# Attention on one NeuronCore: the order of turning and weighting on TensorE

## The chip, the cores and the metric

The program runs on one NeuronCore of a Trainium2 chip. The metric is the device time of one execution in microseconds (us). The engines are TensorE (PE: matmuls and transposes; its weight loads are listed apart as PEld), VectorE (DVE), ScalarE (ACT), GpSimd (POOL) and SyncE (SP, which issues most transfers). Each engine runs its own list of instructions in order, and they meet only at semaphores.

## The reference, cut to what matters

Two layers of cross attention and feed-forward on 2 batches of 512 tokens of width 1024, with a context of 1024 positions. The part that the change touches is the first attention, with 32 heads of width 32 in 8 groups of 4:

```python
scores = jnp.einsum('bghnd,bgsd->bghns', query, key) / D_HEAD ** 0.5
scores = jnp.where(mask, scores, jnp.finfo(scores.dtype).min)
attention = jax.nn.softmax(scores, axis=-1)
out = jnp.einsum('bghns,bgsd->bghnd', attention, value)
out = out.transpose(0, 3, 1, 2, 4).reshape(b, n, D_MODEL)
```

Here n is 512 queries, s is 1024 context positions, h the 4 heads of a group, and b and g together make 16 pairs.

## The kernel before

The kernel runs five stages one after the other. Stage B (`stage_b`, from L596) is the attention, in some 545 of the 1222 us. It goes through 256 steps: 16 pairs (`bg`) of 16 steps each, and a step is one tile of 128 queries of one head against all 1024 positions. A body (`body`) has 32 steps, so two pairs; the first and the last body are written out apart, the six between are a loop. A unit is 8 steps.

For step k the engines do this:

- TensorE computes the scores of step k + 2 (`score`, L689): two matmuls of 512 columns into one of two halves of the PSUM tile `psS`. They run two steps ahead. They wait until VectorE has read the scores that this half held (`masked`).
- VectorE (`mask_min`, L809) adds the mask, writes the tile to SBUF and takes the minimum of each row.
- ScalarE (`exponentials`, L763) takes the exponential and the row sum. This gives the probability tile `Pr`.
- TensorE turns the probability tile, 128 queries by 1024 positions, in eight 128x128 transposes (L736) into the PSUM tile `psT`: first the lower four (half 0), then the upper four (half 1).
- ScalarE copies half 0 out of PSUM (`keep` of ScalarE, L771), VectorE half 1 (`keep` of VectorE, L818), both into `PT`. Half f of step k can only be turned when half f of step k - 1 has been copied (`kept[f]`, wait at L734).
- TensorE weights the values (`weigh`, L703) with the turned tiles of the unit before: one eighth of it in each step, as eight matmuls with 32 columns of weights and 256 moving columns, four side by side in the four column strips of the array. Only the first of the eight portions of a unit waits for anything.
- Once for each pair, in its twelfth step, TensorE spreads the reciprocals of the row sums (`spread_rec`, L715, 32 small matmuls) over the PSUM tile of the output. VectorE multiplies by it two steps later (`normalise`, L830).

TensorE's order in a step is: scores of step k + 2 (S), half 0 (T0), the spreading where there is one, weighting (W), half 1 (T1). VectorE's is: `mask_min` of step k + 2, copy of half 1 of step k. ScalarE's is: exponential of step k + 1, copy of half 0 of step k. In the first eight steps there is nothing to weight, and after the last step eight portions of weighting are left over. Scores are written in steps 0 to 253 alone.

Of the kernel before, what the change touches and what calls it, by code (L numbers as in the profile page):

```python
# [595 lines left out]
def stage_b(nc, ident, hand, QHd, QLd, KHd, KLd, Vd, AOd, early, start_early_loads):  # L596
# [4 lines left out]
    with ExitStack() as stack:  # L601
# [8 lines left out]
        UNIT = 2 * HPG  # L610
# [41 lines left out]
        @block.sync  # L652
        def _(sp):
            def store(bg, u):
                sp.wait_ge(AO_ready, bg + 1)
                sp.dma_start(AOd[ds(bg, 1)].rearrange("a p q -> p (a q)"), AOs[:, u, :]).then_inc(stored[u], 16)


            start_early_loads(sp)
            for u in range(2):  # L660
                sp.wait_ge(hand.stored[u], 32 * (KT + B * KVT))
                sp.wait_ge(hand.q2_stored[u], 16 * NK)
            sp.wait_ge(hand.v_stored, 16 * B)
            with sp.Fori(0, BG // 2 - 1) as it:
                for u in range(2):
                    sp.wait_ge(scored, it * BODY + (u + 1) * STEPS)
                    hand.load_scores(sp, QHd, QLd, KHd, KLd, it * 2 + (u + 2), u)
                    sp.wait_ge(weighed, (it * 2 + (u + 1)) * (STEPS // UNIT))
                    hand.load_values(sp, Vd, it * 2 + (u + 2), u)
                    store(it * 2 + u, u)  # L670
            sp.wait_ge(stored[0], 16 * (GROUPS // 2))
            sp.wait_ge(stored[1], 16 * (GROUPS // 2) + 16)
            for t in range(2):
                early.load_attention(sp, AOd, t)
            for u in range(2):
                store(BG - 2 + u, u)
            sp.wait_ge(stored[0], 16 * (BG // 2))
            sp.wait_ge(stored[1], 16 * (BG // 2) + 16)

        @block.tensor  # L680
        def _(pe):
            def score(it, k):

                u, j = divmod(k, STEPS)
                qt, h = divmod(j, HPG)
                if j == 0:
                    pe.wait_ge(qkv_in[u], (it + 1) * (16 * QKV_DMAS))
                for n in range(2):
                    last = pe.matmul(psS[:, k % 2, n * HALF:(n + 1) * HALF], Qs[:, u, h, qt * P:(qt + 1) * P],  # L689
                                     Ks[:, u, n * HALF:(n + 1) * HALF], start=True, stop=True)  # L690
                last.then_inc(scored, 1)

            def weigh(it, k, first=False):

                u, unit, kt = (k // UNIT - 1) // 2 % 2, k // UNIT - 1, k % UNIT
                if kt == 0:
                    pe.wait_ge(kept[0], it * BODY + k)
                    pe.wait_ge(kept[1], it * BODY + k)
                    if unit % 2 == 0 and not first:
                        pe.wait_ge(AO_ready, it * 2 + (u - 1))  # L700
                cols = slice(unit % 2 * UQ, (unit % 2 + 1) * UQ)
                for h in range(HPG):
                    last = pe.matmul(psO[h * DH:(h + 1) * DH, u, cols], Vs[:, u, kt, :], PT[:, unit % 2, kt, h, :],  # L703
                                     start=(kt == 0), stop=(kt == NK - 1))
                if kt == NK - 1:
                    last.then_inc(weighed, 1)

            def spread_rec(bg, u):

                pe.wait_ge(rec_ready, bg + 1)  # L710
                pe.wait_ge(O_kept, bg + 1)
                for qt in range(QT):
                    for h in range(HPG):
                        one = rec[:, u, qt * HPG + h:qt * HPG + h + 1].to_broadcast([P, DH])
                        last = pe.matmul(psO[h * DH:(h + 1) * DH, u, qt * P:(qt + 1) * P], one, ident[:],  # L715
                                         start=True, stop=True)
                last.then_inc(spread, 1)

            def body(it, first=False, last=False):
                for k in range(BODY):  # L720
                    u, j = divmod(k, STEPS)

                    if not (last and k + 2 >= BODY):
                        pe.wait_ge(masked, it * BODY + (k + 1))
                        if k + 2 < BODY:
                            score(it, k + 2)
                        else:
                            score(it + 1, k + 2 - BODY)
                    pe.wait_ge(probs, it * BODY + (k + 1))
                    for f in range(2):  # L730
                        if f == 1 and not (first and k < UNIT):
                            weigh(it, k, first)
                        if not (first and k == 0):
                            pe.wait_ge(kept[f], it * BODY + k)  # L734
                        for kt in range(NK)[PARTS[f]]:
                            last_t = pe.transpose(psT[:, kt, :], Pr[:, k % PR, kt * P:(kt + 1) * P], ident[:])  # L736
                        last_t.then_inc(turned[f], 1)
                        if f == 0 and j == UNIT + 3 and not (first and u == 0):
                            spread_rec(it * 2 + (u - 1), 1 - u)

            score(0, 0)
            score(0, 1)
            body(0, first=True)
            with pe.Fori(1, BG // 2 - 1) as it:
                body(it)
            body(BG // 2 - 1, last=True)
            for k in range(UNIT):
                weigh(BG // 2, k)
            spread_rec(BG - 1, 1)
# [1351 lines left out]
```

## Time and profile before

| what | us |
|---|---|
| median of 3 runs | 1222.91 |
| lowest and highest of them | 1221.82 and 1226.61 |
| the profiled execution, its own time | 1223.41 |
| its span, first to last instruction | 1221.6 |
| PE busy (86%) | 1052.5 |
| DVE busy (74%) | 903.5 |
| ACT busy (54%) | 658.1 |

The page's row of 40 slices shows TensorE at 9 tenths or more from slice 9 to slice 25, which is the attention. A busy time of TensorE counts modelled ends of matmuls that overlap; so what a group of matmuls costs is better read from one start to the next start. A row with "x4" has merged four instructions that followed each other on the engine.

### The profile page before, as it was taken

Reading aid. Unit: us, or ns where it says so; the run is one execution under the profiler, and the core shown is the slowest. Engines: PE = TensorE matmul, PEld = TensorE weight load, DVE = VectorE, ACT = ScalarE, POOL = GpSimd, SP = SyncE. Lnnn points to the kernel's source line nnn. Section 1 sums busy time; section 2 is a strip of 40 time slices with the busy share of each in tenths; the row PEclk is TensorE's granted clock in tenths of the full one; section 3 lists DMA queues with packets and bytes.
Section 4 is the critical chain, followed back from the end, with each engine's and each line's share of the span. In section 5 each row is a group of like instructions: output and inputs, shape, how many; then the busy total and the mean of one; then the engine's idle time right before and its main releaser. Section 6 shows DMA issues by size and latency. Waiting matters only on the chain. (4 is left out here: it accounts for less than half of the span.)

```text
span 1221.6 us, 21150 instructions
## 1 busy us (share of the span) xinstructions
PE 1052.5 (86%) x7371; PEld 744.7 (61%) x7376; DVE 903.5 (74%) x1886; ACT 658.1 (54%) x1127; POOL 126.0 (10%) x99
## 2 busy tenths in 40 slices
PE   6999997999999999999999999799999877522118
PEld 5878876666666666666666666668888633311007
DVE  5854435989898888888989887646533356699997
ACT  4422211888888888888888886412212074534114
POOL 1211103000000000000000000000112055034300
PEclk9999999999999999999999999899999989855559
DMA  8368887412222221122222210834130000000003
GB/s 336 112 223 293 282 226 247 183 41 66 66 61 64 64 64 44 33 55 64 64 64 60 65 49 10 310 101 124 48 122 0 1 0 1 13 0 0 0 0 138
DMA packets 55566, 112.92 MB, mean 92 GB/s; under 512 B 7724, under 2 KB 21164, under 8 KB 55388
## 3 DMA queue, kind: packets, MB, share of 16 engines
q1 hardware_dynamic: 55452, 112.26, 29.7%
q8 instruction: 30, 0.49, 0.2%
q14 instruction: 20, 0.16, 0.0%
q0 software_dynamic: 64, 0.00, 0.0%
HBM read 83.99 MB, written 27.26 MB: 91 GB/s over the span
## 5 line engine op out<-in xcount | busy, mean ns | idle before, releaser
L763 ACT ACTIVATE XS<-XS,b_mins 128x1024 f32<-128x1024 f32 x256 | 294.9, 1152 | 86.8 <-DVE b_mins L809 84.6
L736 PEld LDWEIGHTS b_psT<-ident,XS 128*128 128x128 f32 x2048 | 235.1, 141 | 144.2 <-issue 100.5
L736 PE MATMUL b_psT<-ident,XS 128*128 128x128 f32 x2048 | 322.2, 281 | 0.8 <-ACT b_PT L771 0.2
L809 DVE CUSTOM_DVE_ANT_0 XS<-b_psS,b_mbias 128x1024 f32<-128x1024 f32 x256 | 312.1, 1219 | 1.7 <-PE b_psS L689 0.6
L818 DVE COPY b_PT<-b_psT 128x512 f32<-128x512 f32 x256 | 177.0, 691 | 54.8 <-PE b_psT L736 53.7
L689 PE MATMUL b_psS<-XTh 128*128 128x512 f32 x512 | 186.3, 446 | 6.6 <-PEq L102 5.5
L703 PE MATMUL b_psO<-b_PT,XTh 128*32 128x256 f32 x2048 | 161.8, 390 | 1.2 <-DVE b_PT L818 0.9
L771 ACT COPY b_PT<-b_psT 128x512 f32<-128x512 f32 x256 | 145.3, 567 | 11.8 <-PE b_psT L736 11.8
L689 PEld LDWEIGHTS b_psS<-XTh 128*128 128x128 f32 x512 | 78.3, 193 | 7.9 <-issue 5.9
L703 PEld LDWEIGHTS b_psO<-b_PT,XTh 128*32 128x32 f32 x2048 | 43.0, 108 | 41.7 <-issue 40.8
L1725 PE MATMUL e_psT<-e_XN,e_dg 128*128 x128 | 30.0, 400 | 41.2 <-DVE XR L1980 41.2
L1147 ACT ACTIVATE c_sd<-c_mv,c_eps 128x1 f32<-128x1 f32 x16 | 4.7, 296 | 103.8 <-DVE c_mv L1234 103.8
L1227 DVE TENSOR_TENSOR XR<-XR,c_psM 128x1024 f32<-128x1024 f32 (+1 forms) x16 | 19.5, 1218 | 55.1 <-PE c_psM L1054 55.1
L399 ACT ACTIVATE a_oh<-a_psM 128x512 fp32r<-128x512 f32 x24 | 14.2, 597 | 82.9 <-PE a_psM L322 62.5
L1295 POOL MEMSET c_eps<- 128x1 f32 x1 | 0.1, 100 | 553.0 <-POOLq L601 553.0
L480 DVE SCALAR_TENSOR_TENSOR a_ol<-a_psM,a_oh 128x512 fp32r<-128x512 f32 x24 | 16.5, 690 | 51.7 <-ACT a_oh L399 51.5
L1725 PEld LDWEIGHTS e_psT<-e_XN,e_dg 128*128 128x128 f32 x128 | 25.8, 202 | 45.8 <-issue 41.9
L1709 PE MATMUL e_psP<-ident,e_xp 128*128 128x128 f32 x16 | 5.5, 448 | 52.8 <-POOL e_xp L2014 52.8
L322 PE MATMUL a_psM<-XTh,WTl 128*128 128x512 f32 x128 | 50.8, 397 | 0.0
L322 PE MATMUL a_psM<-XTh,WTh 128*128 128x512 f32 x128 | 50.7, 396 | 0.0
L1054 PE MATMUL c_psM<-WEh,c_Lh 128*128 128x512 f32 x128 | 50.6, 395 | 0.0
L322 PE MATMUL a_psM<-XTl,WTh 128*128 128x512 f32 x128 | 49.9, 390 | 0.0
(224 smaller groups left out, 1732.8 us busy)
## 6 DMA issues: line engine op xcount, KB each, us to landing
XS<-in_ctx SPq DMA_DIRECT2D x16, 512.0 KB, 5.3
XTh<-QHd SPq DMA_DIRECT2D x32, 256.0 KB, 4.7
XTh<-QLd SPq DMA_DIRECT2D x32, 256.0 KB, 5.2
XS<-in_ctx_turned SPq DMA_DIRECT2D x8, 512.0 KB, 12.0
XS<-in_x SPq DMA_DIRECT2D x8, 512.0 KB, 10.4
a_wst<-in_L_xattn_w_q SPq DMA_DIRECT2D x8, 512.0 KB, 5.5
a_xn<-in_ctx_turned SPq DMA_DIRECT2D x8, 512.0 KB, 3.6
QHd<-a_oh SPq DMA_DIRECT2D x16, 256.0 KB, 4.8
```

Of the source, the lines that this page charges most:

```text
L322: last = pe.matmul(psM[:, m % 4, :], a[:, w % 2, k, :], b[:, k, cols], start=(k == 0 and a is WTh and b is mh), stop=(k == KT - 1 and a is ...
L480: dve.scalar_tensor_tensor(out=ol[:, m % 2, :], in0=psM[:, m % 4, :], scalar=inv_root if M_Q <= m < M_V1 else 1.0, in1=oh[:, m % 2, :].bit ...
L689: last = pe.matmul(psS[:, k % 2, n * HALF:(n + 1) * HALF], Qs[:, u, h, qt * P:(qt + 1) * P], Ks[:, u, n * HALF:(n + 1) * HALF], start=True ...
L703: last = pe.matmul(psO[h * DH:(h + 1) * DH, u, cols], Vs[:, u, kt, :], PT[:, unit % 2, kt, h, :], start=(kt == 0), stop=(kt == NK - 1))
L736: last_t = pe.transpose(psT[:, kt, :], Pr[:, k % PR, kt * P:(kt + 1) * P], ident[:])
L763: act.activation(Pr[:, k % PR, :], Sc[:, k % 4, :], ACT.Exp, bias=mins[:, k % 4:k % 4 + 1], scale=-1.0, accum_out=sums[:, u, j:j + 1]).the ...
L771: act.copy(PT[:, (k // UNIT) % 2, PARTS[0], k % HPG, queries(k)], psT[:, PARTS[0], :]).then_inc(kept[0], 1)
L809: dve.tensor_tensor_reduce(out=Sc[:, k % 4, :], in0=psS[:, k % 2, :], in1=mbias[:, qt, :], scale=1.0, scalar=3.4e38, op0=ALU.add, op1=ALU.min,
L818: dve.tensor_copy(PT[:, (k // UNIT) % 2, PARTS[1], k % HPG, queries(k)], psT[:, PARTS[1], :]).then_inc(kept[1], 1)
L1054: last = pe.matmul(psM[:, u, cols], a[:, u, k, :], w[:, k, cols], start=(k == 0 and i == 0), stop=(k == KT - 1 and i == 2))
L1227: dve.tensor_tensor(row, row, psM[:, u, :], ALU.add).then_inc(added, 1)
L1725: last = pe.matmul(psX(u)[:, i * CH:(i + 1) * CH], dg[:, u, n, i, :], XN[:, ds(t, 1), n * CH:(n + 1) * CH].rearrange("p a n -> p (a n)"), ...
```

## The change

TensorE turns half 0 and half 1 of a tile one after the other, and weights the values after both. The spreading comes after the weighting. Nothing else differs: the same instructions, the same semaphores, the same tiles. The order of a step goes from S, T0, (spreading), W, T1 to S, T0, T1, W, (spreading).

```diff
                     for f in range(2):
-                        if f == 1 and not (first and k < UNIT):
-                            weigh(it, k, first)
                         if not (first and k == 0):
                             pe.wait_ge(kept[f], it * BODY + k)
                         for kt in range(NK)[PARTS[f]]:
                             last_t = pe.transpose(psT[:, kt, :], Pr[:, k % PR, kt * P:(kt + 1) * P], ident[:])
                         last_t.then_inc(turned[f], 1)
-                        if f == 0 and j == UNIT + 3 and not (first and u == 0):
-                            spread_rec(it * 2 + (u - 1), 1 - u)
+                    if not (first and k < UNIT):
+                        weigh(it, k, first)
+                    if j == UNIT + 3 and not (first and u == 0):
+                        spread_rec(it * 2 + (u - 1), 1 - u)
```

## Rows read from the trace of the kernel before

**Rows 1.** Busy time by stretch: stretch, PE, PEld, DVE, ACT, POOL, clock, DMA.
```profile
262.00:296.00 34.00, 34.00 (x322) 22.40 (x321) 30.64 (x51) 27.86 (x50) 0.00 (x0) 1.00 0.25 60
```

**Rows 2.** Timeline of PE in one step: start, us, line, tiles, count.
```profile
401.75 0.72 PE L689 MATMUL b_psS<-XTh 128*128 128x512 f32 x2
402.31 0.60 PE L736 MATMUL b_psT<-ident,XS 128*128 128x128 f32 x4
402.84 0.64 PE L703 MATMUL b_psO<-b_PT,XTh 128*32 128x256 f32 x8
403.41 0.66 PE L736 MATMUL b_psT<-ident,XS 128*128 128x128 f32 x4
403.82 0.72 PE L689 MATMUL b_psS<-XTh 128*128 128x512 f32 x2
```

**Rows 3.** Timeline of the weight loads, the same step.
```profile
402.83 0.16 PEld L703 LDWEIGHTS b_psO<-b_PT,XTh 128*32 128x32 f32 x8 [0.17 <-issue]
403.40 0.42 PEld L736 LDWEIGHTS b_psT<-ident,XS 128*128 128x128 f32 x4 [0.41 <-issue]
403.79 0.30 PEld L689 LDWEIGHTS b_psS<-XTh 128*128 128x128 f32 x2
```

**Rows 4.** Durations by line, ns, min/median/max, 230 to 756 us.
```profile
L736 PEld LDWEIGHTS b_psT<-ident,XS x1976: 137/140/143, 230.5 to 755.5; 128*128 128x128 f32 x198
L736 PE MATMUL b_psT<-ident,XS x1976: 270/272/331, 230.5 to 755.6; 128*128 128x128 f32 x198
...
L689 PEld LDWEIGHTS b_psS<-XTh x490: 190/191/192, 232.1 to 752.1; 128*128 128x128 f32 x164
```

**Rows 5.** Waits between 230 and 756 us: total, times, longest.
```profile
PEld b_psT L736 <- issue: 99.1, 247, 0.5
...
PEld b_psT L736 <- DVE b_PT L818: 6.2, 15, 0.4
```

**Rows 6.** Timeline of PE in stage C, just after matmuls with 40 columns (L1078).
```profile
802.75 0.50 PE L1054 MATMUL c_psM<-WOh,c_Lh 128*128 128x512 f32 x1
803.08 0.39 PE L1054 MATMUL c_psM<-WOl,c_Lh 128*128 128x512 f32 x1
```

**Rows 7.** Timeline of DVE and ACT around the step of rows 2.
```profile
402.11 0.69 DVE L818 COPY b_PT<-b_psT 128x512 f32<-128x512 f32 x1 [0.27 <-PE b_psT L736]
402.72 1.22 DVE L809 CUSTOM_DVE_ANT_0 XS<-b_psS,b_mbias 128x1024 f32<-128x1024 f32 x1
403.86 0.08 DVE L809 DVE_READ_ACCUMULATOR2_ANT b_mins<- 128x1 f32 x1
...
403.98 1.15 ACT L763 ACTIVATE XS<-XS,b_mins 128x1024 f32<-128x1024 f32 x1 [0.34 <-DVE b_mins L809]
```

**Rows 8.** Timeline in the first eight steps, where nothing is weighted.
```profile
217.04 1.20 PE L689 MATMUL b_psS<-XTh 128*128 128x512 f32 x2
218.44 1.23 DVE L809 CUSTOM_DVE_ANT_0 XS<-b_psS,b_mbias 128x1024 f32<-128x1024 f32 x1 [0.32 <-PE b_psS L689]
...
226.79 0.69 DVE L818 COPY b_PT<-b_psT 128x512 f32<-128x512 f32 x1
227.00 0.95 PEld L736 LDWEIGHTS b_psT<-ident,XS 128*128 128x128 f32 x8 [0.52 <-ACT XS L763]
```

**Rows 9.** Timeline of DVE around a `normalise`.
```profile
277.42 0.68 DVE L830 TENSOR_TENSOR b_AOs<-b_psO,b_Os 128x512 f32<-128x512 f32 x1
```

**Rows 10.** Timeline at the end of the last step.
```profile
756.03 0.63 PE L736 MATMUL b_psT<-ident,XS 128*128 128x128 f32 x4 [0.16 <-ACT b_PT L771]
757.16 0.66 PE L736 MATMUL b_psT<-ident,XS 128*128 128x128 f32 x4
757.85 0.69 DVE L818 COPY b_PT<-b_psT 128x512 f32<-128x512 f32 x1 [1.25 <-PE b_psT L736]
...
758.66 0.83 PEld L703 LDWEIGHTS b_psO<-b_PT,XTh 128*32 128x32 f32 x20 [1.08 <-issue]
```

## The prediction

> **What bounds the kernel now.** I read the busy times by stretch first. Through the attention TensorE is busy all the time at full granted clock (2.4 GHz), VectorE about 90% and ScalarE 82% [rows 1]. Busy PE is not yet proof of a bound, so the second view is TensorE's timeline of one step [rows 2]. From starts: S to T0 0.56 us, T0 to W 0.53, W to T1 0.57, T1 to the next S 0.41; together 403.82 - 401.75 = 2.07 us. The third view, the waits, says whether any of that is another engine's fault: the load of T1 stands idle 0.41 us before it, 247 times, released by "issue", that is by nothing the profile shows [rows 5]. The 15 waits there put down to VectorE's copy are the same 0.4 us each; so they aren't a wait that a new order could remove. The copy that T1 needs ended at 402.11 + 0.69 = 402.80, 0.6 us before T1 loads at 403.40 [rows 3, 7]. So TensorE alone sets the pace here, and what counts is how long its own list takes. Some 248 of the 256 steps have this form.
>
> **What the switches cost now.** Four transposes after scores are busy 0.60 us with the last one lasting 0.272, so they stand (0.60 - 0.272) / 3 = 0.109 us apart and four take 0.436 [rows 2, 4]. T0 to W takes 0.53, 0.09 more than that. The weighting's first load starts at 402.83, after the last transpose has streamed (402.31 + 0.44 = 402.75): it isn't pulled ahead [rows 2, 3]. On the way out the transposes' load starts at 403.40, with 0.41 us without any load before it, and the four transposes are busy 0.66 us in place of 0.60, the longest single one 331 ns in place of 272: some 57 ns of the first one's load stand bare [rows 2 to 4]. All other loads are hidden: that of the scores follows T1 without a gap [rows 3]. So a step has two drains, full array to strips and strips to full array, and after the second one a bare load.
>
> **The change part by part.**
>
> *T0 and T1 together.* No drain and no bare load between them. The bounds for the seam are 0 and 0.04: in the first eight steps, where the halves already follow each other, the eight loads take 0.95 us against 7 x 0.109 + 0.14 = 0.90, and the rest is the wait for VectorE's copy, which ended at 226.79 + 0.69 = 227.48, just when T1 could start [rows 8]. That wait isn't there when the copy is early (below), so I take 0. T8 to W is then 0.53 + 0.436 = 0.97 us.
>
> *W moved behind T1.* The drain into the strips is the same 0.09, at another place. The drain out is the same, too: W to the next first matmul 0.57. But what follows is now the scores, and their load is longer: 191 ns against 140 [rows 4]. In this stage it is never bare. The nearest row is in stage C, where a matmul of the same shape follows matmuls on part of the columns: it lasts 0.50 against 0.39 for the next, and the next starts 0.33 to 0.34 us later [rows 6]. So 0.11 bare in place of 0.057. By starts: S to T0 becomes 0.335 + 0.24 = 0.575 (0.24 is the pace of a score matmul, (402.31 - 401.75 with the 0.08 that the last transpose still holds taken off) / 2), against 0.56. The step: 0.575 + 0.97 + 0.57 = 2.113, that is +0.040. By bare loads: 0.11 - 0.057 = +0.05, less the 0.006 by which the scores come late behind T1 now: +0.044. I take +0.042. Its ends are 0 (the load costs no more than the transposes' does, -0.006 at best) and +0.054 (0.50 - 0.39 = 0.11 bare, less 0.057, with no discount).
>
> *How often.* A score behind a weighting occurs after steps 8 to 252: 245 times. 245 x 0.042 = +10.3 us.
>
> *The copies.* Both copies are still released by their half and needed one step later, so each has a whole step less its own four transposes. VectorE's place in the step moves, though: T1 is now ready 0.6 us earlier against the scores. VectorE goes mask_min, copy, mask_min. The copy takes 0.61 to the next start and mask_min 1.14 [rows 7]: 1.75 of 2.11 us, so 0.36 of slack. A mask_min that waits for scores starts 0.19 us after their modelled end (218.44 against 217.04 + 1.20) [rows 8]. In the new order, with S starting at 0, the scores end at 0.335 + 0.40 = 0.74, mask_min starts at 0.93, and the copy behind it at 2.07, which is 0.04 before the next S. It ends at 0.65 of that step; with 0.05 for the semaphore 0.70. T1's load is due at 0.575 + 0.436 - 0.11 = 0.90. Slack 0.20 us: T1 isn't late. `normalise` puts up to 0.68 between copy and mask_min [rows 9], where VectorE would otherwise stand 0.93 - 0.57 = 0.36 us: mask_min late by up to 0.32, which is 0.12 over the slack. 15 x 0.12 makes at most +1.8 us in all, and 0 at least; what starts next on VectorE overlaps the end of the one before it (0.61 and 0.69 for the copy), so I take 0. The exponential starts 0.12 us after mask_min's last row (403.98 against 403.86) [rows 7], in the new order right at an S, and ScalarE has 2.11 us for it and a copy that together take 82% of a step now [rows 1]; the turning of that tile starts over 1 us after it ends. Nothing waits.
>
> *The waits in the weighting, and the spreading.* The first portion of a unit waits for both copies of the step before; T0 and T1 now stand before it and have waited for the same. The spreading (15 of 16) stays beside the weighting, so no further switch; its reader comes two steps later. I cost both at 0, ends -0.03 and +0.05 x 15, as half a us. Behind them are queued only the next scores, which are two steps ahead. Of the queue of transfers, the load of the next values waits for the weighting of a unit, now 0.4 us later; it is needed seven steps (14 us) on. 0.
>
> *The end.* The last weighting waits for the last copy of half 1, which starts at 757.85, 0.69 us after T1's first transpose at 757.16; the weighting starts 0.81 later at 758.66 [rows 10]. In the new order T1 starts at 756.03 + 0.44 = 756.47 and the portion that lay ahead of it fills the wait: the copy starts at 757.16 and the weighting at 757.97. -0.7 us, once.
>
> **The sum.** +10.3 - 0.7 = +9.6 us. Against the profiled execution's own 1223.41 that is 1233.0; that execution lies 0.5 us above the median, so against the median 1232.5.
>
> **The rivals.**
>
> *A: the score's bare load costs no more than the transposes'.* Then the step is as long as before (2.07, or 0.006 less), and only the end is won: -0.7 - 1.5, about 1221. For it: both loads fill 128 columns of the array, and TensorE takes them for the same shape. Against it: 191 and 140 ns, and the 0.11 of stage C. It decides below +0.02 a step. The Trainium skill (TensorE: Matmul & The Clock Gate, LDWEIGHTS) prices a load by its columns alone, which is this rival; the trace's 191 against 140 ns for the same 128 columns disagrees. 13%.
>
> *B: the score's load is pulled ahead into the weighting.* Then the drain (0.09) and the load (0.11) behind W both go: 2.11 - 0.20, so -0.16 x 245 = -39 us, 1184. Against it: the load of T1, whose semaphore had long been there, has never gone ahead of W, 247 times [rows 5]. The Trainium skill (TensorE Tiling, Key Properties) says that a change of the tiling mode drains the engine; by this rule, too, nothing goes ahead, and the trace agrees with 0.41 us without a load. 3%.
>
> *C: VectorE becomes the bound.* Its way from S over mask_min (0.93 + 1.14), copy and semaphore (0.74) to T1's load, and from there over W to the S after it (2.11 - 0.90 = 1.21) takes 4.02 us for two steps of 4.23. If VectorE sees the scores 0.3 us later than I reckon, a step is 0.05 longer again: +12 us, 1245. It decides from 0.21 on. 8%.
>
> *D: a gain from copies that start earlier,* which is what the order suggests: VectorE now stands 0.27 us before its copy [rows 7]. It is worth nothing as long as TensorE waits for no copy, which is so; 0.02 a step at most, 5 us, 1218. 3%.
>
> **How the numbers follow.** The forecast with its own range, 1229 to 1237, gets 70%, A 13%, C 8%, B 3%, D 3%, and 3% are left for what I don't see. For 8 times in 10 the range must reach A and part of the way to C: 1220 to 1240. A measurement of this kernel can tell about 0.5%, 6.1 us, from no change: over 1229.0 is slower, under 1216.8 faster. The forecast is 3.5 us over that bound, so a tenth of it goes to "same". Slower 0.63 + 0.08 + 0.04 = 0.75, same 0.07 + 0.13 = 0.20, faster 0.05.
>
> **What would show it.** In the changed kernel's timeline: S to T0 0.575, T x8 to W 0.97, W to S 0.57, the step 2.11; the first score matmul of a step at about 0.50 us; the 0.41 us without a load now before L689 and none before T1; VectorE's idle time before mask_min, released by the scores, and none before the copy. The prediction is wrong if the step is under 2.09, if the load before L689 has no idle time, or if T1 waits for VectorE's copy.

## The result and the profile after

The changed kernel takes 1230.5 us (median of 20 runs) where the kernel before takes 1223.7 (20 runs of the same comparison). The ratio is 1.0056, 95% interval 1.0044 to 1.0068: slower by 6.8 us. The forecast was +9.6 us, or 1232.5 us.

The profiled execution of it took 1234.69 us, 11 more than that of before. Of these, 4.2 us lie ahead of the attention: its first score matmul starts at 215.3 us, against 211.0. The change can't cause that, and in a second profile of the same kernel (below) it starts at 211.9. From its first score matmul to the start of its last spreading matmul, the last of the stage, the attention takes 552.9 us before, 559.0 and 558.9 in the two profiles after. So it is +6.0 to +6.1 us in this stage. What lies behind it takes 457.7 us before and 458.6 in both profiles after; the kernels of the experiments, which leave that part alone, spread over 3 us there, so this difference isn't read as one of the change.

The timeline of TensorE after, to be read against [rows 2]:

```profile
404.12 0.73 PE L689 MATMUL b_psS<-XTh 128*128 128x512 f32 x2
404.68 1.03 PE L734 MATMUL b_psT<-ident,XS 128*128 128x128 f32 x8
405.65 0.64 PE L703 MATMUL b_psO<-b_PT,XTh 128*32 128x256 f32 x8
406.22 0.50 PE L689 MATMUL b_psS<-XTh 128*128 128x512 f32 x1
```

From starts: S to T0 0.56 us, eight transposes to W 0.97, W to S 0.57. The step is 406.22 - 404.12 = 2.10 us, 0.027 more than before at the precision of the trace (2.100 against 2.073). The weight loads of the same step, against [rows 3]:

```profile
404.11 0.30 PEld L689 LDWEIGHTS b_psS<-XTh 128*128 128x128 f32 x2 [0.41 <-issue]
404.45 1.02 PEld L734 LDWEIGHTS b_psT<-ident,XS 128*128 128x128 f32 x8
405.64 0.16 PEld L703 LDWEIGHTS b_psO<-b_PT,XTh 128*32 128x32 f32 x8 [0.17 <-issue]
```

The 0.41 us without a load has moved from the transposes' load to the scores', and the 0.17 ahead of the weighting's load has stayed. No load of the transposes stands still in mid-step any more. VectorE, against [rows 7]:

```profile
402.96 1.23 DVE L809 CUSTOM_DVE_ANT_0 XS<-b_psS,b_mbias 128x1024 f32<-128x1024 f32 x1 [0.27 <-PE b_psS L689]
404.11 0.08 DVE L809 DVE_READ_ACCUMULATOR2_ANT b_mins<- 128x1 f32 x1
404.11 0.69 DVE L818 COPY b_PT<-b_psT 128x512 f32<-128x512 f32 x1
405.06 1.23 DVE L809 CUSTOM_DVE_ANT_0 XS<-b_psS,b_mbias 128x1024 f32<-128x1024 f32 x1 [0.27 <-PE b_psS L689]
```

VectorE no longer waits before its copy but before mask_min, for the scores: it starts 405.06 - 404.12 = 0.94 us after them. The waits between 230 and 760 us, against [rows 5]:

```profile
PEld b_psS L689 <- issue: 96.2, 241, 0.4
...
DVE XS L809 <- PE b_psS L689: 65.5, 198, 1.1
...
PEld b_psT L734 <- DVE b_PT L818: 0.2, 1, 0.2
```

The first row is the drain, now in front of the scores in 241 steps. The last says that half 1 waited for VectorE's copy once in this stretch, for 0.2 us. The end of the last step, against [rows 10]:

```profile
767.08 1.06 PE L734 MATMUL b_psT<-ident,XS 128*128 128x128 f32 x8
...
768.18 0.69 DVE L818 COPY b_PT<-b_psT 128x512 f32<-128x512 f32 x1 [0.95 <-PE b_psT L734]
...
769.02 2.53 PE L703 MATMUL b_psO<-b_PT,XTh 128*32 128x256 f32 x41 [0.31 <-DVE b_PT L818]
```

From the last half 0 to the weighting left over: 769.02 - 767.08 = 1.94 us, before 758.69 - 756.03 = 2.66 (the weighting's matmuls there start at 758.69, 0.03 after their load). That is the -0.7 us of the forecast.

### The profile page after: what moved, and what is told of

Read it like the earlier page. It is cut to its first block and busy times, and to the rows that moved or that the text cites. A ratio compares the mean times of both kernels' runs of the same rounds, so it can differ in the third digit from the quotient of the medians.

```text
span 1232.9 us, 21155 instructions
## 1 busy us (share of the span) xinstructions
PE 1064.8 (86%) x7376; PEld 760.4 (62%) x7376; DVE 894.0 (73%) x1886; ACT 659.0 (53%) x1127; POOL 126.4 (10%) x99
## 5 line engine op out<-in xcount | busy, mean ns | idle before, releaser
L734 PE MATMUL b_psT<-ident,XS 128*128 128x128 f32 x2048 | 268.5, 274 | 0.9 <-DVE b_PT L818 0.3
L734 PEld LDWEIGHTS b_psT<-ident,XS 128*128 128x128 f32 x2048 | 240.0, 141 | 39.3 <-ACT XS L763 2.8
```

## The experiments

A drain is the stretch without a weight load at a change between the full array and its strips. A load is bare where no matmul runs beside it, so that it costs time. The theory: TensorE's own list sets the pace, and the step grew because the matmul behind the weighting's drain, whose load stands bare, is now a score with a longer load. The rivals: the two halves without a break cost the time; the later spreading does; a chain through VectorE does.

### Only the spreading moved

```diff
                         if f == 1 and not (first and k < UNIT):
                             weigh(it, k, first)
+                        if f == 1 and j == UNIT + 3 and not (first and u == 0):
+                            spread_rec(it * 2 + (u - 1), 1 - u)
...
-                        if f == 0 and j == UNIT + 3 and not (first and u == 0):
-                            spread_rec(it * 2 + (u - 1), 1 - u)
```

> Only the second half of the change: the order of a step is scores, half 0, weighting, (spreading), half 1. The theory that the time went to the score's bare load behind the weighting says that nothing changes here: 15 spreadings stay next to the weighting, no load and no drain is added, +-0.5 us, a step of 2.07 us. A rival, that the later spreading delays the normalising and so VectorE, would give 15 times up to 0.5 us, so up to +7 us, which is the whole loss.

Measured: ratio 0.9999 (0.9983 to 1.0014), 1224.4 us against 1224.8; the step 2.073 us, the stage 553.2 us against 552.9. So the second half of the change costs nothing that can be told, and the loss belongs to the first. The interval alone leaves room for 2 us either way; the stage and the step are what narrow it.

### Both halves together, but behind the weighting

```diff
+                    if not (first and k <= UNIT):
+                        weigh(it, k - 1, first)
+                    if j == UNIT + 3 and not (first and u == 0):
+                        spread_rec(it * 2 + (u - 1), 1 - u)
                     pe.wait_ge(probs, it * BODY + (k + 1))
...
-                    if not (first and k < UNIT):
-                        weigh(it, k, first)
-                    if j == UNIT + 3 and not (first and u == 0):
-                        spread_rec(it * 2 + (u - 1), 1 - u)
...
+            weigh(BG // 2, -1)
             for k in range(UNIT):
                 weigh(BG // 2, k)
```

> Both halves are turned without a break, as in the changed kernel, but the weighting stands between the scores and the halves and is one step late, so that a transpose follows it and no score matmul: scores, weighting of the step before, (spreading), half 0, half 1. The bare-load theory expects the step of the kernel before or 0.006 less (2.067 to 2.073 us), and 1221 to 1224 us, against 2.100 us and +6.8 us of the changed kernel. A rival, that the two halves without a break, or copies that are released together, cost the time, expects about 2.10 us a step and +6 us or more.

Measured: ratio 0.996 (0.9944 to 0.9975), 1220.1 us against 1224.8: 4.7 us faster than the kernel before, and some 10 faster than the changed one. TensorE's timeline of a step:

```profile
402.74 0.72 PE L689 MATMUL b_psS<-XTh 128*128 128x512 f32 x2
403.39 0.64 PE L703 MATMUL b_psO<-b_PT,XTh 128*32 128x256 f32 x8
403.96 1.09 PE L738 MATMUL b_psT<-ident,XS 128*128 128x128 f32 x8
404.81 0.48 PE L689 MATMUL b_psS<-XTh 128*128 128x512 f32 x1
```

The step is 404.81 - 402.74 = 2.07, exactly 2.067 us. The eight transposes have no break here either, and W to the next group is the same 0.57 us. The load of the scores is hidden again, behind the last transpose: half 0 to the scores takes 0.85 us, the way from eight transposes to a group with a hidden load. Two things tell this kernel from the changed one: what comes after the drain, and what stands ahead of the weighting, scores in place of transposes. The second costs under 0.01 us by the starts: the weighting follows the last score after 0.327 us, 0.09 to 0.10 more than a score's pace of 0.228 to 0.237, and in the changed kernel it follows the last transpose after 0.202, 0.09 more than a transpose's 0.109. So the 0.033 us a step go with the load behind the drain, and the rival that turning without a break costs the time has fallen.

The stage is 3.8 us shorter than in the kernel before, and little of that is the common step. The 22 odd steps there, of 2.10 to 2.20 us, give 1.7 us, all the other steps from the twelfth on 0.9, the first eleven steps 0.9 and the end 0.3. Here 228 steps last 2.07.

### The weighting of two steps at once

```diff
-                        if f == 1 and not (first and k < UNIT):
-                            weigh(it, k, first)
+                        if f == 1 and k % 2 == 1 and not (first and k < UNIT):
+                            weigh(it, k - 1, first)
+                            weigh(it, k, first)
```

> The order of the kernel before, but the weighting of two steps is done together in every second step, so half as many changes between the full array and its strips. If each round trip costs two drains and a bare load of the transposes, 0.09 + 0.03 + 0.09 + 0.06 = 0.26 us, then two steps take 0.26 us less: 124 times, -32 us at most. VectorE needs 1.75 us a step on its own, and a step without weighting takes TensorE only 1.35, so a wait for the copy of half 1 is to be expected there; worked out as some 0.1 us in two steps, -20 us then. A rival, that VectorE's and ScalarE's order lets no gain through when TensorE's steps are uneven, expects 2.07 us a step on average and no change.

Measured: ratio 0.9855 (0.9835 to 0.9875), 1206.2 us against 1224.8, 18 us faster.

```profile
401.44 0.71 PE L689 MATMUL b_psS<-XTh 128*128 128x512 f32 x2
401.99 1.14 PE L737 MATMUL b_psT<-ident,XS 128*128 128x128 f32 x8
402.88 0.72 PE L689 MATMUL b_psS<-XTh 128*128 128x512 f32 x2
403.44 0.60 PE L737 MATMUL b_psT<-ident,XS 128*128 128x128 f32 x4
403.97 1.07 PE L703 MATMUL b_psO<-b_PT,XTh 128*32 128x256 f32 x16
404.97 0.66 PE L737 MATMUL b_psT<-ident,XS 128*128 128x128 f32 x4
405.38 0.48 PE L689 MATMUL b_psS<-XTh 128*128 128x512 f32 x1
```

Two portions take 1.00 us, one takes 0.57: the second costs 0.43, so 0.14 of the 0.57 is the way out of the strips, and the 0.09 on the way in comes on top. Two steps last 405.38 - 401.44 = 3.94 us against 4.15. The gain is 0.21 and not 0.26: eight transposes to the next scores take 0.89, where eight that follow scores take 0.79 if nothing waits (403.59 - 402.80 in the next experiment). The 0.10 is the wait for VectorE's copy that the expectation had worked out: half 1 of the first of the two steps starts 0.06 us after that copy's end (402.47 against 401.72 + 0.69, its load then bare). The number of switches is worth more here than all that the change moves.

### The same pairs in the changed order

```diff
-                    if not (first and k < UNIT):
-                        weigh(it, k, first)
+                    if k % 2 == 1 and not (first and k < UNIT):
+                        weigh(it, k - 1, first)
+                        weigh(it, k, first)
```

> The order of the changed kernel, with the weighting of two steps together behind half 1 in every second step. The bare load and drains are halved in number: 0.31 us less in two steps than the changed kernel if nothing else binds, 4.20 - 0.31 = 3.89. Against the kernel with pairs in the order before it should be longer by the difference of the two loads, 0.03 to 0.05 us in two steps, some 5 us, unless the copies bind.

Measured: ratio 1.0281 (1.0259 to 1.0302), 1258.4 us. The expectation, with 3.89 us for two steps, failed by far: two steps last 4.43. TensorE and VectorE:

```profile
402.23 0.73 PE L689 MATMUL b_psS<-XTh 128*128 128x512 f32 x2
402.80 1.03 PE L734 MATMUL b_psT<-ident,XS 128*128 128x128 f32 x8
403.59 0.72 PE L689 MATMUL b_psS<-XTh 128*128 128x512 f32 x2
404.17 0.63 PE L734 MATMUL b_psT<-ident,XS 128*128 128x128 f32 x4
405.07 0.66 PE L734 MATMUL b_psT<-ident,XS 128*128 128x128 f32 x4 [0.28 <-DVE b_PT L819]
405.66 1.07 PE L703 MATMUL b_psO<-b_PT,XTh 128*32 128x256 f32 x16
406.66 0.50 PE L689 MATMUL b_psS<-XTh 128*128 128x512 f32 x1
```

```profile
403.18 1.23 DVE L810 CUSTOM_DVE_ANT_0 XS<-b_psS,b_mbias 128x1024 f32<-128x1024 f32 x1 [0.85 <-ACT XS L764]
404.33 0.08 DVE L810 DVE_READ_ACCUMULATOR2_ANT b_mins<- 128x1 f32 x1
404.33 0.69 DVE L819 COPY b_PT<-b_psT 128x512 f32<-128x512 f32 x1
```

This is the chain of rival C in the prediction, here as the bound: scores at 402.23, mask_min 0.95 later, 1.15 until the copy, 0.74 until half 1 of the next step can start at 405.07, and 1.59 over half 1 and the weighting to the scores at 406.66: 4.43 us for two steps. The 0.85 us ahead of mask_min are put down to ScalarE, but of ScalarE mask_min needs only the exponential of four tiles earlier, which was long done, and it starts with the usual 0.95 behind the scores; so it waited for them. The whole weighting lies behind half 1 and ahead of the scores, so it lengthens the chain. In the order of the kernel before it lies ahead of half 1, where VectorE works beside it.

### Pairs behind the scores

```diff
+                    if k % 2 == 0 and not (first and k <= UNIT):
+                        weigh(it, k - 2, first)
+                        weigh(it, k - 1, first)
                     if j == UNIT + 3 and not (first and u == 0):
                         spread_rec(it * 2 + (u - 1), 1 - u)
                     pe.wait_ge(probs, it * BODY + (k + 1))
```

> Pairs of weightings once more, but between the scores and half 0 of every second step (scores, weighting of the two steps before, half 0, half 1), with the spreading one step earlier so that it stays beside a weighting. The chain from a step's scores over mask_min and the copy of half 1 to half 1 of the next step, which bound the pairs behind half 1, starts right before the weightings here, so they lie inside it and cost nothing. Expected as with pairs between the halves, 3.94 us for two steps, 1203 to 1207 us. If the copy of half 1 binds in the short step by more than there (both short distances, half 0 to half 0 and half 1 to half 1, now lie in the same step), up to 4.05 and 1218.

The kernel that ran left the spreading in the twelfth step, where there is no weighting; the expectation says otherwise. Measured: ratio 0.9831 (0.9809 to 0.9853), 1203.9 us against 1224.6, inside the expected 1203 to 1207. Then with the spreading really one step earlier:

```diff
-                    if j == UNIT + 3 and not (first and u == 0):
+                    if j == UNIT + 2 and not (first and u == 0):
```

> The kernel with pairs of weightings between scores and half 0, now with the spreading one step earlier, so that it stands right behind a pair. In the run before it stood in a step of its own without a weighting: scores to spreading 0.64 and spreading to half 0 1.01 us, against 0.57 from scores to half 0 without it, 1.08 us each. Behind a pair it should cost 0.46 + 0.99 - 0.57 = 0.88 us. So 15 x 0.20 = 3 us less than 1203.9, about 1201. If the normalising of VectorE, not the extra switch, makes these steps long, no change.

Measured: ratio 0.9811 (0.9792 to 0.9829), 1200.8 us against 1224.5, 23 us faster than the kernel before. The stage is 2.9 us shorter than in the run before it (529.8 against 532.7), as 15 switches saved at 0.20 us should make it. Its timeline:

```profile
402.24 0.72 PE L689 MATMUL b_psS<-XTh 128*128 128x512 f32 x2
402.81 1.11 PE L739 MATMUL b_psT<-ident,XS 128*128 128x128 f32 x8
403.68 0.71 PE L689 MATMUL b_psS<-XTh 128*128 128x512 f32 x2
404.32 1.07 PE L703 MATMUL b_psO<-b_PT,XTh 128*32 128x256 f32 x16
405.32 0.88 PE L739 MATMUL b_psT<-ident,XS 128*128 128x128 f32 x6
```

### How much slack each order leaves VectorE

```diff
+        JUNK = 128
+        junk = sb("b_junk", [P, 4, JUNK])
...
+                    dve.tensor_copy(junk[:, k % 4, :], ident[:, 0:JUNK])
                     keep(it, k, first)
```

> The kernel before with one more instruction of VectorE in each step, a copy of 128x128 from SBUF to SBUF between mask_min and the copy of half 1, estimated at 0.15 to 0.3 us. In this order a step's chain scores, mask_min, copy, half 1 of the next step has 0.9 us of slack over two steps; what is left is VectorE's own time, 1.75 + 0.15 to 0.3 = 1.90 to 2.05 us of 2.07. So no change, or up to +3 us through the steps with a normalising.

> The changed kernel with the same extra instruction d of VectorE. The chain from the scores over mask_min (0.94 + 1.15) and the copy with its semaphore (0.74) to half 1 of the next step, and over the weighting to the next scores (1.21), is 4.04 + d over two steps of 4.20. With d = 0.15 nothing changes, with d = 0.3 two steps take 4.34, +17 us over the changed kernel; so the changed kernel loses more by this instruction than the kernel before. If the chain is not what counts, both lose the same.

Measured: in the kernel before 1.0019 (1.0005 to 1.0032), 2 to 3 us; in the changed kernel 1.0078 (1.0058 to 1.0098) against the kernel before, 1234.3 us, so about +4 over the changed kernel. By the stage alone it is +3.4 and +4.1 us. One such copy takes 0.13 us to the next start, two take 0.27. The common steps stayed at 2.07 and 2.10; those after a normalising grew, to 2.31 and 2.40 us, and some of the first eleven. This doesn't tell the two orders apart. With two such copies in each step:

```diff
-                    dve.tensor_copy(junk[:, k % 4, :], ident[:, 0:JUNK])
+                    for i in range(2):
+                        dve.tensor_copy(junk[:, k % 2 * 2 + i, :], ident[:, 0:JUNK])
```

> The kernel before with two extra copies of 128x128 on VectorE in each step, between mask_min and the copy of half 1. One took 0.14 us from start to next start, so two make d = 0.27. VectorE's own time is 1.74 + 0.27 = 2.01 of 2.07 us, and the chain scores, mask_min, copies, half 1 has 0.9 us of slack over two steps. Expected: the common step still 2.07 us; the steps around the 15 normalisings longer by some 0.3 us each, 3 to 8 us in all over the kernel before.

> The changed kernel with the same two copies. Its chain from the scores over mask_min (0.94 + 1.15), d = 0.27, copy and semaphore (0.74) to half 1 of the next step and over the weighting to the scores after it (1.21) is 4.04 + 0.27 = 4.31 us for two steps of 4.20. If that chain is the second bound, the common step becomes 2.15 us, +12 us and the normalisings' 4 us over the changed kernel. If only VectorE's own time counts, the step stays at 2.10 us and only the normalisings cost.

Measured: 1.0078 (1.0055 to 1.0100) in the kernel before, its common step still 2.07 us; 1.0173 (1.0150 to 1.0195) in the changed kernel, 1245.5 us, so 15 over the changed kernel. By the stage alone: 552.9 to 561.0 (+8.1, expected 3 to 8), and 558.9 to 574.8 (+15.9, expected 16). The common step of the second is no longer 2.10:

```profile
400.65 0.73 PE L691 MATMUL b_psS<-XTh 128*128 128x512 f32 x2
...
402.76 0.73 PE L691 MATMUL b_psS<-XTh 128*128 128x512 f32 x2
403.33 1.08 PE L736 MATMUL b_psT<-ident,XS 128*128 128x128 f32 x8
...
404.91 0.73 PE L691 MATMUL b_psS<-XTh 128*128 128x512 f32 x2
```

Two steps last 404.91 - 400.65 = 4.26 us against the 4.31 that the chain was worked out to, with half 1 late inside the eight transposes (1.08 busy in place of 1.03). In the kernel before, the same two copies left the common step where it was. So the change has not only made the step longer, it has also put VectorE's chain within some 0.2 us in two steps of the bound.

### The changed kernel once more

> The changed kernel once more, unchanged, beside the others on the same chip and for a second profile of it. Expected 2.100 us a step and 1230.5 us, with the first stage as long as in the kernel before (in the first profile it was 4 us longer, which the change can't cause).

Measured: 1.0049 (1.0029 to 1.0070), 1230.3 us, step 2.100, first scores at 211.9 us. The extra 4 us ahead of the attention in the first profile are not the change's.

## Why the prediction was right, and where its size was off

**The bound.** Right: TensorE sets the pace. Its common step moved with its own neighbours alone, in the changed kernel and with the weighting behind the scores. VectorE's chain took over only with the pairs behind half 1 (4.43 us) and with two more copies in the changed kernel.

**The drains.** Right: as many as before, one of them moved. Halving their number, with nothing else changed but when a portion is weighted, gives 18 us. The Trainium skill (TensorEngine Tiling (Array Packing), Key Properties) says that changing the tiling mode drains the engine. The trace agrees: 0.17 us without a load ahead of the weighting and 0.41 behind it, before and after the change (and 0.37 ahead of it in the kernel where it follows the scores).

**The bare load.** Right in kind. With a transpose behind the drain the step is 2.067 us, with a score 2.100, and the other difference between the two lists costs under 0.01. That it is the load, and not something else about a score that follows a drain, rests on sizes: the load behind the drain is recorded at 0.186 us for the scores and 0.139 for the transposes, 0.047 apart, and the first score holds its successor back 0.335 us in place of 0.228 (+0.107), the first transpose 0.166 in place of 0.109 (+0.057), 0.050 apart. No run changes the load alone. The Trainium skill (TensorE: Matmul & The Clock Gate, LDWEIGHTS) prices a load by its columns alone; by that rule both steps would be equal, and the measurement decides against it. Rival A falls with it.

**Its size.** This is the term that was off: +0.042 us a step was forecast, +0.027 measured. Two things went wrong in it. First, the working by starts took 0.575 us from S to T0, and it is 0.567: the two scores start 0.335 apart, as taken from stage C, but the second one then lasts 0.232 us and not the 0.24 read from a step before. The rest are roundings, 0.97 for 0.964 and 0.57 for 0.569. As printed, this sum gives 2.115 and not 2.113 us, so +0.042 and not +0.040, where 2.100 was measured. Second, the working by bare loads (+0.044) set one load against the other and left the scores' own pace as it was. But without its bare 0.107 the first score takes 0.335 - 0.107 = 0.228 us, and the second 0.232, where the step before gives 0.237 for each. That is 0.009 and 0.005, together 0.014 of the 0.017 us by which this working was too high. 245 x 0.027 = 6.6 us.

**Nothing else waits.** Nearly: the slack of half 1 against VectorE's copy was 0.20 us by forecast; the copy ends at 404.11 + 0.69 = 404.80, 0.05 goes to the semaphore, and half 1's first load is due at 404.68 + 0.44 - 0.11 = 405.01, so 0.16. Around the normalisings the step is 2.13 us in place of 2.10, 14 times: +0.4 us, inside the bounds of 0 and 1.8 and taken at 0. One more step, near the end, lasts 2.30: the 0.2 us that half 1 waited. mask_min starts 0.94 us after the scores (0.93).

**The end.** -0.7 us, as forecast. These terms add up to 6.6 + 0.4 - 0.7 = +6.3 us; the stage shows +6.0 to +6.1, the medians +6.8.

**The spreading and the waits in the weighting.** The spreading at nothing: right, by the run that moved it alone. The waits in the weighting were costed at nothing, and that is not what the traces show. In the kernel before, 22 steps last 2.10, 2.15 or 2.20 us, together 1.5 us over the common one; at the same places the changed kernel has 2.100 to 2.105. Six of them, at 2.20, are steps in which a unit's first portion starts, and they lose their time right ahead of it: its load starts 0.32 us after the last transpose in place of 0.20, and 0.24 us after the end of VectorE's copy that it waits for. In the changed kernel that copy has ended over 0.8 us before. The copy alone isn't the cause, as in other units the load follows it by 0.12 us and nothing is lost; what comes on top there, and what makes the other sixteen steps long, is open.

So the near agreement of 6.3 with 6.0 is in part luck. The change also won these 1.5 us, and it lost about as much in places that no term names: 0.6 us in the 47 steps around the spreadings that lasted 2.06 in the kernel before, 0.3 in the first eleven steps, 0.2 in the step of 2.30, and 0.1 in steps a few ns over 2.100. With these the sum is 6.3 - 1.5 + 1.2 = +6.0 us.

**Rival D,** the gain from copies that start earlier: VectorE's copy does start without waiting, and it is worth nothing in the common step, as no half waited for it there. If the six steps of 2.20 us are its doing, it is worth 0.8 us in all. Rival B is excluded by the 241 drains before the scores.

## What to carry to other kernels

On an engine that runs its list without waiting, a new order is worth what it changes between neighbours: count the changes between full-array and strip matmuls, and see which weight load comes right after each, since here that one wasn't hidden. Put the matmul with the shortest load there, and gather the strip matmuls into fewer, longer groups; here that gave 23 us, where the order within a step alone gave -5 or +7. Before such work is moved, follow the chain through the second busiest engine: the same pairs are 18 us faster where VectorE works beside them, and 34 us slower where they lie in its chain.

## What the runs showed of the hardware

A weight load of 128 columns takes 190 ns in the records for the scores (fp32r) and 140 ns for the transposes (fp32). Two orders that differ in which of the two follows the drain are 0.033 us a step apart, as if this difference counted once the load is bare. The load behind the weighting was not pulled ahead into it: about 0.4 us passed without a load in the 241 listed places before the scores and the 247 before the transposes. Why the pace of the score matmuls itself moves between 0.228 and 0.237 us with the order is open; no run was made on it.
